# Second cross attention of a decoder kernel: TensorE's order inside a pair of heads

## The reference

```python
def _L1_xattn_ref(key, query, mask, w_q, w_k, w_v, w_o):   # NH = 16, D = 64
    q = jnp.einsum('blj,njd->bnld', query, w_q)
    k = jnp.einsum('blj,njd->bnld', key, w_k)
    v = jnp.einsum('blj,njd->bnld', key, w_v)
    score = jnp.einsum('bnid,bnkd->bnik', q, k) / sqrt_d
    m = mask[:, None]
    score = score * m + NEG * (1.0 - m)
    attn = jax.nn.softmax(score, axis=-1)
    out = jnp.einsum('bnij,bnjk->bnik', attn, v)
    return jnp.einsum('bnlj,njk->blk', out, w_o)
```

## Time and profile before

| what | value |
|---|---|
| median of 3 runs (lowest, highest) | 1765.83 us (1758.49, 1766.81) |
| the profiled execution: its time | 1767.52 us |
| the profiled execution: its span, first to last instruction | 1765.8 us |
| TensorE busy, share of the span | 1315.4 us, 74% |
| VectorE busy | 1426.4 us, 81% |
| ScalarE busy | 1101.4 us, 62% |
| GpSimd busy | 1140.0 us, 65% |
| mean granted clock of TensorE | 0.883 |
| second cross attention, scores of the first pair to the end of the output projection | 1392.3 to 1692.0 us of the span |

### The profile page before, as it was taken

The page is one execution under the profiler, slowest core; times in us unless marked ns, Lnnn a source line. Parts: engine busy times, 40 slices in busy tenths (PEclk is TensorE's granted clock), DMA queues, the critical chain, the costliest instruction groups (busy, mean ns, idle before and its releaser), DMA issues. The chain is left out here.

```text
span 1765.8 us, 23296 instructions
## 1 busy us (share of the span) xinstructions
PE 1315.4 (74%) x6904; PEld 648.2 (37%) x6907; DVE 1426.4 (81%) x2430; ACT 1101.4 (62%) x2435; POOL 1140.0 (65%) x742
## 2 busy tenths in 40 slices
PE   6777898986757656767567666667746799899979
PEld 4554565553322212222122222212201465566543
DVE  4654898978259999999999999999996477777845
ACT  4444887876566566676566666566644577777740
POOL 2101565651079999999999999999994144444410
PEclk9999999998878888798888888888867799999989
DMA  3000000000054453353443443543332311111000
GB/s 102 1 1 2 1 2 1 1 20 7 6 223 164 190 191 133 132 207 138 191 186 145 145 186 137 198 186 145 121 136 80 111 49 49 48 72 72 1 1 24
DMA packets 70215, 168.03 MB, mean 95 GB/s; under 512 B 20420, under 2 KB 40152, under 8 KB 56664
## 3 DMA queue, kind: packets, MB, share of 16 engines
q1 hardware_dynamic: 68680, 166.17, 25.6%
q10 hardware_dynamic: 1168, 0.53, 0.1%
q0 software_dynamic: 256, 0.01, 0.0%
HBM read 131.04 MB, written 35.65 MB: 94 GB/s over the span
## 5 line engine op out<-in xcount | busy, mean ns | idle before, releaser
L1633 POOL TENSOR_TENSOR ma_hs<-ma_dtuR,ma_Bt 128x1024 f32<-128x1024 f32 x256 | 596.6, 2358 | 7.0 <-DMA ma_dtuR<-ma_dtu_d 6.7
L1816 ACT ACTIVATE ps<-ma_dtR,ma_A 128x512 f32<-128x512 f32 x512 | 332.7, 682 | 297.2 <-DVE ma_hs L1961 254.8
L845 POOL TENSOR_TENSOR x_pr<-x_pr,x_rec 128x512 f32<-128x512 f32 x256 | 267.4, 1045 | 291.6 <-DVE x_rec L1085 291.6
L1955 DVE TENSOR_TENSOR_SCAN ps<-ps,ma_hs 128x1024 f32<-128x1024 f32 x176 | 401.5, 2281 | 0.2
L1710 PE MATMUL ps<-ma_hs,ma_fold 128*32 128x512 f32 x1024 | 174.7, 816 | 206.1 <-POOL ma_hs L1641 177.4
L1051 ACT ACTIVATE x_pr<-x_sm,x_mx 128x256 f32<-128x256 f32 x512 | 255.2, 500 | 68.9 <-DVE x_mx L1076 65.9
L1961 DVE TENSOR_TENSOR ma_hs<-ps,ma_Ct 128x1024 f32<-128x1024 f32 x176 | 215.4, 1224 | 6.1
L1955 DVE TENSOR_TENSOR_SCAN ma_hs<-ps,ma_hs 128x1024 f32<-128x1024 f32 x80 | 182.5, 2281 | 18.3 <-ACT ps L1816 15.4
L1641 POOL TENSOR_TENSOR ma_hs<-ma_hs,ma_Ct 128x1024 f32<-128x1024 f32 x80 | 188.2, 2353 | 12.3 <-DVE ma_hs L1955 12.1
L1677 PE MATMUL ps<-ma_hn,ma_w_tap 128*128 128x512 f32 (+3 forms) x256 | 142.0, 707 | 52.4 <-ACT ma_hn L1840 52.4
L907 PE MATMUL ps<-ident,x_pr 128*128 128x128 f32 x1024 | 163.2, 286 | 5.4 <-DVE x_pT L985 4.4
(11 more groups left out here) (304 smaller groups left out, 2168.6 us busy)
## 6 DMA issues: line engine op xcount, KB each, us to landing
ma_dtuR<-ma_dtu_d SPq DMA_DIRECT2D x32, 1024.0 KB, 6.7
ma_dtR<-ma_dt_d SPq DMA_DIRECT2D x32, 1024.0 KB, 8.7
ma_Bt<-ma_bc_d SPq DMA_DIRECT2D x16, 1024.0 KB, 5.0
ma_Ct<-ma_bc_d SPq DMA_DIRECT2D x16, 1024.0 KB, 7.4
ma_dtu_d<-ma_dtu SPq DMA_DIRECT2D x32, 256.0 KB, 2.0
ma_dt_d<-ma_dt SPq DMA_DIRECT2D x32, 256.0 KB, 2.3
keys_d<-ma_kv SPq DMA_DIRECT2D x32, 256.0 KB, 4.4
values_d<-ma_kv SPq DMA_DIRECT2D x32, 256.0 KB, 2.5
```

The lines of the kernel that those rows point to most:

```text
L845: pool.tensor_tensor(pr[:, r, :, :], pr[:, r, :, :], rec[:, r, :].unsqueeze(2).broadcast_to([P, 2, L]), ALU.mult).then_inc(pr_done, 1)
L1633: pool.tensor_tensor(hs[:, k % SLOTS, :, :], dtuR[:, unit(f, h), q, :].unsqueeze(1).broadcast_to([P, 2, CH]), rows(Bt, k), ALU.mult).then_ ...
L1816: e = act.activation(c.ps[:, 2 * (k % 2) + a, :], dtR[:, unit(f, h), q, :], ACT.Exp, scale=A[:, (f // QUARTERS) % 2, h, q, no:no + 1])
L1955: dve.tensor_tensor_scan(out, pair(k), slot(k), 0.0, ALU.mult, ALU.add).then_inc(scan_done, 1)
```

## The change

For the second cross attention alone, `step` issues the values' product first and then, at even n, the turns of heads n-4 and n-3 together; at odd n it issues nothing. And `step` now stands ahead of the query projections and the output projection in the body of the loop. For the first cross attention nothing moves. No other engine's queue is touched.

```diff
--- before.py
+++ after.py
@@ -954,21 +954,29 @@
                     project(0, n, True, False)
 
                 def step(b, p, n, first):
-                    for a, b_, p_, f in late(n, LAG, b, p, first):
-                        turn(b_, a, f)
+                    if small:
+                        for a, b_, p_, f in late(n, LAG, b, p, first):
+                            turn(b_, a, f)
                     for g, b_, p_, f in groups(n, b, p, first):
                         weigh(b_, p_, g, f)
+                    if not small and n % 2 == 0:
+                        for i in (n, n + 1):
+                            for a, b_, p_, f in late(i, LAG, b, p, first):
+                                turn(b_, a, f)
 
                 def body(b, p, fresh, first, last):
                     for n in range(NH):
                         if n % 2 == 0:
                             score_pair(b, p, n, first)
+                        if not small:
+                            step(b, p, n, first)
                         if not last:
                             for a in units(n):
                                 project(b + 1, a, False, first)
                         if n == LAG + 3 and not first:
                             out_projection(b, fresh, False)
-                        step(b, p, n, first)
+                        if small:
+                            step(b, p, n, first)
                 looped(pe, body)
                 for n in range(NH, NH + LAG + 1):
                     step(B - 1, 1, n, False)
```

## The result

The changed kernel takes 1782.6 us (median of 4 runs, 1781.3 to 1784.5); before, 1763.9 us in the runs on the same chip (1758.5 to 1766.8, 4 runs). The ratio is 1.0104, with a 95% interval of 1.0078 to 1.0129: slower by 18.7 us. The prediction had 1785 in 1775 to 1803, 19 us above the median that it started from.

The account below looks back on a forecast made before the run. The second cross attention was taken as bound by neither TensorE nor VectorE alone, with ScalarE's fixed queue the chain at risk. 1767.5 + 18 + 1 = 1786.5 us profiled, 1785 against the median of 1765.8; range 1775 to 1803.

Parts of the forecast that it names:

- The walk: Timing of pairs 8 to 14 in a second cross attention batch, instruction by instruction: next pair 0 about 2.5 us late.
- What bounds the stage: Second cross attention: neither TensorE alone nor VectorE alone; TensorE idle 21.6 us over seven batches, waiting for VectorE's masked product.
- The main term: Pairs 8 to 14: products wait for ScalarE's copies held behind late projections; 2.6 us in each of seven batches, +18.
- The two turns back to back: TensorE's two turns together take 1.09 us against 1.16 apart; 0.06 saved per pair, 3.8 us for the stage.
- Pairs without projections: Pairs with no query projections: product still covered by the turned head's copy, 0 to 0.1 us each; 0.1 from pairs 0 to 6.
- Pair 14: Last pair of a batch: starts 2.45 us late, its product waits 0.65, next pair 0 begins about 2.5 late.
- The wait in all: New wait of values' products for ScalarE's copies: about 3.3 us a batch, 25 us in all.
- End of the stage: After the last scores, turns of later heads stand behind products waiting for copies: between 0 and 2 us, taken as +1.
- Order is free: Rival: ScalarE catches up within each pair, no product waits, only shorter turns count; 1762 us, chance 0.07.
- partly hidden: Rival: only pair 12's delay survives, pairs led by VectorE absorb the rest; about 1 us a batch, 1774, chance 0.13.
- The clock falls: Rival: pair 12's new wait drops TensorE's granted clock, 1.6 us more in each of seven batches; 1796, chance 0.16.
- Reductions run free: Rival: GpSimd's product moves past VectorE's reduction, 8 us come back plus 3.8 of turns; 1754, chance 0.04.

Follow-up runs that it names:

- e3: Changed kernel, with ScalarE's copies of the query projections moved behind the exponential of the same head: +3.4 us against the kernel before, ratio 1.0017.
- e6: Changed kernel, with its four query projections spread one each over four pairs, last in each pair: +36.0 us against the kernel before, ratio 1.0209.
- e7: Changed kernel, with query projections spread over four pairs and ScalarE's copies of them behind the exponential: +5.2 us against the kernel before, ratio 1.0023.
- e1: Changed kernel, with products first and turns together, but query and output projections left where they were before: +4.7 us against the kernel before, ratio 1.0026.
- e8: Changed kernel, with ScalarE's copies of the projections between turned copy and exponential of the same head: +9.6 us against the kernel before, ratio 1.0069.
- e5: Kernel before, with its four query projections spread one each over four pairs (heads 8, 10, 12, 14): -8.5 us against the kernel before, ratio 0.9951.
- e2: Kernel before, with turns and product moved ahead of the projections but in their old order: +6.2 us against the kernel before, ratio 1.0028.
- e4: Kernel before, with ScalarE's copies of the query projections moved behind the exponential of the same head: +10.5 us, ratio 1.0063.

## Why the prediction was right, point by point

The mechanism is the forecast one, and its signs came: waits of the product in pairs 10, 12 and 14, late exponentials, a batch of 38.80 us (38.9 forecast). That the total agrees so closely, 18.7 against 19, is partly luck. In the traces the stage grew by 16.3 us, 17 without the clock's fall in the kernel before, where the forecast had 19 in the stage and nothing outside it. The walk was 2 to 3 us too high, and the medians happen to differ by about as much more than the stage does.

- **What bounds the stage.** Right. TensorE's waits for VectorE moved from 27.2 to 24.6 us, and pairs 0 to 4 kept their 4.29, 4.07 and 3.66 us.
- **The main term**, +18 in seven batches. The mechanism is shown by e3, e6 and e7. Its size was a little high: over the seven batches the starts are 254.4 us apart before and 269.7 after, so +15.3, or +16.1 without the fall of the clock in the kernel before. A usual batch went from 36.48 to 38.80, +2.32 where the step said 2.6. Pair by pair, the walk gave pair 10 a wait of 0.95 and it was 0.82; pair 12 1.78, and it was 1.57; pair 14 0.65, and it was 0.72. ScalarE's idle time before the first and the last projection was 4.73 and 2.19, where the prediction had "more than 4" and "about 2.5".
- **The two turns back to back** were mis-sized, and this is most of what was too high. The step took 1.09 us from the end of the stage, or 1.12 in the walk; that row's length holds the pipeline's tail. From start to next start, inside a batch, the two take 0.93 (1523.64 to 1524.57), where apart each took 0.53 behind a projection and 0.58 elsewhere. So the saving is 0.13 in pair 8 and about 0.2 in the others, and not 0.06. It made pair 8 shorter than before (5.86 against 5.94), where the walk had 6.00. Pair 12 began 10.72 us after pair 8, where the walk had 11.12, and the turns of two pairs, 0.19 less each, make 0.38 of these 0.40. Pairs that end in a wait for VectorE can't keep the saving.
- **Pairs without projections**, 0.1: it was 0.13, all in pair 6, where the product waited 0.25 for its copy.
- **Pair 14** went the other way: the walk gave it 4.1 us, and it took 4.34, 0.27 more than before. e1 and e3 have it at 4.34 and 4.33 too, so this part belongs to the product's place and not to the late copies, to which the walk had put it.
- **The wait in all.** Forecast 25 us, measured 29.0: the waits of 0.25 and 0.28 in pairs 6 and 0 were not in the walk. Busy time was to stay; TensorE's fell by 8.6 us (1315.4 to 1306.8), and that of the rows of the turns by 13.0 (163.2 to 150.2).
- **End of the stage**, +1: from the last batch's first scores to the end, 45.3 us before and 46.4 now, +1.1.
- **GpSimd, DMA.** Costed at zero, and right: TensorE's weight loads before a turn wait 9.6 us for GpSimd's product in all, against 10.8, and nothing waits for a DMA.
- **The rivals.** "Order is free" and "partly hidden" fell with the result. "The clock falls" did not happen in the waits that the change made: the product behind the wait of 1.57 us runs at its full-clock 1.08, and the granted clock of the batch is 1.00:

```profile
1502.00:1541.00 39.00, 32.86 (x227) 22.32 (x225) 28.92 (x104) 26.78 (x85) 17.02 (x17) 1.00 0.15 55
```

  Nor did it in e6, where such waits reach 1.74 us and the products behind them take 1.08. Past the first batch the kernel before has one fall, after a wait of 1.86 us; the changed kernel has none. The fall makes the stage before some 0.8 us longer than it need be, so the change costs about 17 us in the stage rather than 16.3. That wait was itself lengthened by the slow instruction of the last section; the same instruction gave waits of 1.65 to 1.67 us in the traces of the changed kernel, e1, e3 and e8, and no fall. Early in the first batch, behind waits of 2.42 and 2.45 us, the scores take 2.08 us instead of 1.13 in both kernels alike.
- "Reductions run free" did not happen either: the reductions of the second cross attention (L1076, now L1084) take 111.2 us in all, against 110.4 before.
- **The rule of the Trainium skill** (Perfetto Trace Analysis, Matmul Optimizations), to issue matmuls back to back in batches, was followed by the change and did give TensorE 0.13 to 0.2 us a pair. The measurement decides: the granted clock was 1.00 in these batches before and after, so there was none to gain, and each batch became 2.3 us longer, because ScalarE, which copies the results out, was held up. The order of e5, which breaks the batch of three projections up, is the faster one.

What stays open: e1 and e2 sum to about 11 of 19 us. That the rest is their interaction on ScalarE's queue agrees with the walk and with e3, but no run turns that interaction on by degrees. The 2.4 us that the medians have over the stage's growth are not explained.

## What to carry to other kernels

When a producer's pieces are reordered, look at the consumer's queue, and reorder it with them if need be. An engine that copies results out in a fixed order will sit before the one that now comes last, and everything behind it in its queue, here the turned copies and the exponentials, is late, though the engine is idle a quarter of the time or more (ScalarE is busy 26.8 of 36 us). Work that is free to move belongs where the bound is another engine, in small portions; with ScalarE's queue as it stands, at the head of the group (e5, -8.5 us) and not at its end (e6, +36.0). A new wait in a trace is no loss by itself: half of the product's wait stayed in e3, at +3.4 us. And a block's cost on TensorE is read from start to next start; the length of the last instruction holds a tail that the next one hides.

## What the runs showed that I had not expected

One instruction of VectorE, the shift of the mask at a batch's start, usually takes 0.43 us, and 0.93 to 1.32 us once or twice in eight of the ten traces, with the same operands. GpSimd's rows beside it tell why. The usual case, in the kernel before:

```profile
1500.59 1.32 POOL L845 TENSOR_TENSOR x_pr<-x_pr,x_rec 128x512 f32<-128x512 f32 x1 [0.79 <-DVE x_rec L1085]
1500.59 0.43 DVE L1130 TENSOR_SCALAR x_neg<-x_m 128x512 f32 x1
```

and the slow one, in the same trace:

```profile
1573.54 1.04 POOL L845 TENSOR_TENSOR x_pr<-x_pr,x_rec 128x512 f32<-128x512 f32 x1 [0.79 <-DVE x_rec L1085]
1573.55 1.31 DVE L1130 TENSOR_SCALAR x_neg<-x_m 128x512 f32 x1
```

One of the two instructions waits for the other, and the one that starts first seems to win. The shift stands beside GpSimd's product of `pr` in each of seven batches of all ten traces. In 57 of these 70 cases the shift takes its 0.41 to 0.43 us, and the product ends 0.89 or 0.90 later and takes 1.14 to 1.33 us instead of 1.04. In the other 13 the product takes its 1.04, and the shift ends 0.27 or 0.28 later. In 9 of the 13 the shift starts 0.07 to 0.39 us behind the product, and in none of the 57 does it start more than 0.01 behind; in the other 4, and in many of the 57, the starts are too close for the trace to part them. No run moves the shift away from the product, so this rests on the rows alone.

The slow case makes pair 0 of its batch 0.9 us longer (5.18 instead of 4.29), except in e7, where two of them changed nothing: there pair 0 takes 3.63 us with or without. The traces of e2 and e4 have none. The batches of the table are free of it; the stages and the medians are not, so differences of a microsecond or two between stages may be its work. The main one, 16.3 us, has it once on either side.
